# Mixture-of-experts layer in split float32: the shared down product of 30 steps, four of its five token tiles in pairs by seven block products, placed between the two routed up products

## The reference, cut to what matters

```python
x = x + gnn(layernorm(x)) + linear_attention(layernorm(x))      # 625 tokens, width 1024
xn = layernorm(x)
# 8 experts, the best 2 of each token, at most 97 tokens (CAP) each:
gate = silu(einsum('ech,ehi->eci', xg, rg)); up = einsum('ech,ehi->eci', xg, ru)   # i = 4096
eout = einsum('eci,eih->ech', gate * up, rd)
routed = zeros.at[dispatch].add(eout * w)
shared = silu(xn @ sg) * (xn @ su) @ sd                          # i = 8192, all 625 tokens
x = x + shared + routed
```

## Time and profile before

| | |
|---|---|
| median of 3 runs | 2823.61 us (2823.45 to 2825.22) |
| span of the profiled execution | 2825.1 us |
| PE busy | 2804.8 us (99% of the span), 14886 matmuls |
| DVE busy | 2233.2 us (79%) |
| ACT busy | 1489.3 us (53%) |
| DMA | 549 MB, mean 194 GB/s, 56% of the 16 engines' time |

### The profile page before, as it was taken

The page is one execution under the profiler, slowest core; times in us unless marked ns, Lnnn a source line. Parts: engine busy times, 40 slices in busy tenths (PEclk is TensorE's granted clock), DMA queues, the critical chain, the costliest instruction groups (busy, mean ns, idle before and its releaser), DMA issues.

```text
span 2825.1 us, 40627 instructions
## 1 busy us (share of the span) xinstructions
PE 2804.8 (99%) x14886; PEld 2317.9 (82%) x14886; DVE 2233.2 (79%) x2735; ACT 1489.3 (53%) x1941; POOL 55.4 (2%) x73
## 2 busy tenths in 40 slices
PE   9999999999999999999999999999999999999999
PEld 8975898788888888888888888888888888888877
DVE  8847256988888888888888888888888888888888
ACT  7722233555555555555555555555555555555563
POOL 0010000000000000000000000000000000000001
PEclk9999999999999999999999999999999999999999
DMA  4020131766666666666666666666666666666676
GB/s 114 15 83 30 60 105 45 228 217 223 223 236 223 217 212 234 222 217 214 218 214 213 215 226 211 218 216 229 219 216 216 225 219 219 224 223 217 220 263 233
DMA packets 270275, 549.06 MB, mean 194 GB/s; under 512 B 16673, under 2 KB 82465, under 8 KB 269927
## 3 DMA queue, kind: packets, MB, share of 16 engines
q1 hardware_dynamic: 265954, 532.11, 55.8%
q0 software_dynamic: 3936, 14.06, 1.6%
q10 hardware_dynamic: 162, 0.08, 0.0%
HBM read 537.49 MB, written 8.70 MB: 193 GB/s over the span
## 4 chain that ended last, share of the span: by engine, by line
PE 95%; DVE 3%; issue 0%; DMA 0%; ACT 0%; POOL 0%; POOLq 0%; DVEq 0%; SPq 0%; ACTq 0%
PE ps L1892 26%; PE ps L1896 26%; PE ps L1895 26%; PE ps L1660 3%; PE ps L1697 2%; PE ps L1699 2%; PE ps L1698 2%; PE ps L1750 2%; PE ps L1943 1%; PE ps L1784 1%; PE ps L1782 1%; PE ps L1783 1%; DVE C L990 0%; DVE c_lo L1087 0%; PE ps L1792 0%
## 5 line engine op out<-in xcount | busy, mean ns | idle before, releaser
L1439 DVE TENSOR_TENSOR c_lo<-raw,c_hi 128x1024 fp32r<-128x1024 f32 x832 | 985.1, 1219 | 99.8 <-ACT c_hi L809 99.4
L809 ACT CAST c_hi<-raw 128x1024 fp32r<-128x1024 f32 x832 | 862.9, 1050 | 157.1 <-PE ps L1896 156.7
L1892 PE MATMUL ps<-tok_hi,c_hi 128*128 128x314 f32 x1792 | 552.9, 309 | 2.8 <-DVEq L1627 1.7
L1896 PE MATMUL ps<-tok_hi,c_lo 128*128 128x314 f32 x1792 | 552.0, 308 | 0.0
L1895 PE MATMUL ps<-tok_lo,c_hi 128*128 128x314 f32 x1792 | 551.8, 308 | 0.0
L1892 PE MATMUL ps<-c_hi,xgT_hi 128*97 128x512 f32 x1024 | 404.6, 395 | 0.0
L1896 PE MATMUL ps<-c_hi,xgT_lo 128*97 128x512 f32 x1024 | 404.1, 395 | 0.0
L1895 PE MATMUL ps<-c_lo,xgT_hi 128*97 128x512 f32 x1024 | 403.3, 394 | 0.0
L1505 DVE TENSOR_TENSOR resid<-ps,resid 125x512 f32<-125x512 f32 x320 | 218.9, 686 | 178.4 <-PE ps L1896 178.2
L1892 PEld LDWEIGHTS ps<-tok_hi,c_hi 128*128 128x128 f32 x1792 | 339.4, 189 | 5.7 <-issue 1.8
L1895 PEld LDWEIGHTS ps<-tok_lo,c_hi 128*128 128x128 f32 x1792 | 339.8, 190 | 1.4
(11 more groups left out here) (251 smaller groups left out, 3526.2 us busy)
## 6 DMA issues: line engine op xcount, KB each, us to landing
raw<-in_L_ffn_rg SPq DMA_DIRECT2D x256, 512.0 KB, 4.8
raw<-in_L_ffn_ru SPq DMA_DIRECT2D x256, 512.0 KB, 4.7
raw<-in_L_ffn_rd SPq DMA_DIRECT2D x256, 512.0 KB, 6.2
raw<-in_L_ffn_sg SPq DMA_DIRECT2D x64, 512.0 KB, 5.4
raw<-in_L_ffn_su SPq DMA_DIRECT2D x64, 512.0 KB, 5.5
raw<-in_L_ffn_sd SPq DMA_DIRECT2D x64, 512.0 KB, 5.7
wl<-in_L_mix_w_qkv SPq DMA_DIRECT2D x6, 2048.0 KB, 7.9
wl<-in_L_gnn_W SPq DMA_DIRECT2D x2, 2048.0 KB, 23.1
```

The source lines that it names most:

```text
L809: nc.scalar.copy(c_hi[u % RING][:], raw_at_(q, r)[:]).then_inc(sem("hi_done"), 1 + (U - UNITS) * (u == UNITS - 1))
L1439: V.tensor_tensor(c_lo[u % RING][:], raw_at_(q, r)[:], c_hi[u % RING][:].bitcast(F32), ALU.subtract).then_inc(sem("lo_done"), 1 + (U - UNI ...
L1892: m = MM(out_, l_hi, r_hi, start=first, stop=False, skip_group_check=skip)
L1896: return MM(out_, l_lo, r_hi, start=False, stop=last, skip_group_check=skip)
```

## The change

In the 30 STEP steps:

- Token tiles 0 and 1, and 2 and 3, form two pairs. For each pair the 2 by 2 block product (two token tiles, two groups of 128 inner columns, two halves of 512 output columns) is done by seven products in place of eight. Tile 4 is done plainly, in 4 products. So there are 18 products, 54 matmuls, where there were 20 and 60.
- The factors of the scheme: DVE makes four sums of `h` (`inner_sums`, 128 by 250 each, into `hs`) and four sums of halves of the `sd` weights in the raw buffers (`down_sums`, 128 by 512 each). The shared down product has four units in place of two (15 to 18), so a step has 35. Rounding `h` goes from DVE to ACT (`inner_hi`, `inner_sums_hi`), and the subtractions are `inner_lo` and `inner_sums_lo`.
- Partial results are copied from bank to bank by ACT (`down_seed`, six of 125 by 512). One product of each pair belongs to two outputs; it is summed on its own in `p7` over all steps (`p7_add`, two of 125 by 512 a step), and the last step adds it to the odd tiles' `resid`. The ten additions to `resid` stay, as `down_add`.
- The place: the shared down product runs between `routed_up(0)` and `routed_up(1)`. `turn_inner(0)` comes between the two halves of `routed_up(1)`, then `routed_down(0, 4)`, then `turn_inner(1)`, then `routed_down(4, 8)`.
- Loads are reordered to suit; the buffers `hs`, `hs_hi`, `hs_lo` and `p7` lie where part of the descriptors' scratch area was.

Its core:

```diff
-STEP = Order(s=0, gate=(7, 15), sd=23, rd=25, a_bank=(A0, R0))
+STEP = Order(s=0, gate=(7, 19), sd=15, rd=27, a_bank=(A0, X0), sd_units=4)
@@ loads
-            blocks = {STEP: shared + inner + over + down, FIRST: shared + over + inner + down,
+            blocks = {STEP: shared + inner[0:8] + over + inner[8:16] + down, FIRST: shared + over + inner + down,
@@ ACT, hi
+                if order is STEP and u in (order.sd + 2, order.sd + 3):
+                    act.wait_ge(sem("down_sums"), count(e, q, 4, 2 * (u - order.sd - 1)))
@@ ACT, down_seed(n)
+                act.wait_ge(sem("down_ps"), count(e, q, 16, (D_P1A, D_P1B, D_P6A, D_P6B, D_P5A, D_P5B)[n]))
+                if n in (2, 3):
+                    act.wait_ge(sem("sd_added"), count(e, q, 2 * NT, (2, 1)[n - 2] + ONE))
+                if n in (4, 5):
+                    act.wait_ge(sem("p7_added"), count(e, q, 2, n - 3))
+                nc.scalar.copy(PS[to][0:TP, :], PS[DOWN_A[p]][0:TP, :]).then_inc(sem("down_seeded"), 1)
@@ ACT, step
-            for u in range(14, 21):
+            inner_hi(0)
+            inner_hi(1)
+            hi(14)
+            inner_sums_hi()
+            for u in range(15, 17):
                 hi(u)
             silu_routed(0)
-            for u in range(21, 30):
+            for u in range(17, 22):
+                hi(u)
+            down_seed(0)
+            down_seed(1)
+            hi(22)
+            for n in range(2, 6):
+                down_seed(n)
+            for u in range(23, 30):
                 hi(u)
             turned_hi(0)
             silu_routed(1)
+            for u in range(30, 32):
+                hi(u)
             turned_hi(1)
-            for u in range(30, 33):
+            for u in range(32, 35):
                 hi(u)
@@ DVE, step
-            shared_inner(1)
-            for u in range(13, 21):
+            shared_mult(1)
+            inner_sums()
+            lo(13)
+            inner_lo(0)
+            inner_lo(1)
+            lo(14)
+            inner_sums_lo()
+            for u in range(15, 17):
                 lo(u)
+            down_sums()
             routed_inner(0)
-            for u in range(21, 27):
+            for u in range(17, 20):
                 lo(u)
-            for n in range(2 * NT):
-                shared_add(n)
-                ...
+            down_add(DOWN_LAST[0], D_TA, NT - 1, 0)
+            lo(20)
+            down_add(DOWN_LAST[1], D_TB, NT - 1, 1)
+            p7_add(0)
+            p7_add(1)
+            lo(21)
+            for p in range(2):
+                down_add(DOWN_B[p], (D_P2A, D_P2B)[p], 2 * p, 0)
+            lo(22)
+            ...
+            for u in range(23, 30):
+                lo(u)
+            turned_lo(0)
+            routed_inner(1)
+            for u in range(30, 32):
+                lo(u)
             turned_lo(1)
-            for u in range(30, 33):
+            for u in range(32, 35):
                 lo(u)
@@ PE, step
             routed_up(0)
-            pe.wait_ge(sem("s_up"), count(e, q, 4, 4 + ONE))
-            routed_up(1)
+            shared_down_products()
+            pe.wait_ge(sem("sd_added"), count(e, q, 2 * NT, 5 + ONE))
+            routed_up(1, (0,))
             pe.wait_ge(sem("h_done"), count(e, q, 2, 1 + ONE))
+            pe.wait_ge(sem("sd_added"), count(e, q, 2 * NT, 2 * NT + ONE))
             turn_inner(0)
-            pe.wait_ge(sem("sh_ready"), count(e, q, 2, 2 + ONE))
-            for n in range(2 * NT):
-                shared_down(n)
+            routed_up(1, (1,))
+            routed_down(0, 4)
             pe.wait_ge(sem("h_done"), count(e, q, 2, 2 + ONE))
             turn_inner(1)
-            routed_down(0, 8)
+            routed_down(4, 8)
```

More of the change, by code:

```diff
@@ L124, in __init__ @@
         self.last_unit = [self.at(last[b - self.b0]) if self.b0 <= b < self.b0 + 4 else
-                          next(u for u in range(UNITS) if not self.shared(u) and self.block(u) == b)
+                          max(u for u in range(self.units) if not self.shared(u) and self.block(u) == b)
                           for b in range(BLK)]
@@ L143, in block @@
     def block(self, u):
[L145 removed]
+        if u <= self.s:
+            return u
+        if u < self.sd + 2 or self.sd_units == 2:
+            return u - (NPROD - 4)
+        return u - (NPROD - 4) - 2
     def raw(self, u):
@@ L482, in _, with step @@
             sp.dma_start(d, v).then_inc(sem(f"wl_in{n % 2}"), 16)
-        def step(e, q, order=STEP, part=slice(None)):
+        def step(e, q, order=STEP, part=slice(None), before=STEP):
             gate, up = sg_v[e * Q + q], su_v[e * Q + q]
@@ L509, in _ @@
         for q in range(1, Q):
-            step(0, q)
+            step(0, q, before=FIRST if q == 1 else STEP)
         with sp.Fori(1, E - 1) as e:
@@ new lines, in down_add, with p7_add @@
+            def down_add(bank, at, t, half):
+                r = resid[:, t, half * HALF:(half + 1) * HALF]
+                dve.wait_ge(sem("down_ps"), count(e, q, 16, at))
+                V.tensor_tensor(r, PS[bank][0:TP, :], r, ALU.add).then_inc(sem("sd_added"), 1)
+            def p7_add(p):
+                dve.wait_ge(sem("down_ps"), count(e, q, 16, (D_P7A, D_P7B)[p]))
+                V.tensor_tensor(p7[:, p, :], PS[DOWN_D[p]][0:TP, :], p7[:, p, :], ALU.add).then_inc(sem("p7_added"), 1)
@@ L1514, in step @@
                     lo(u)
+                for p in range(2):
+                    for half in range(2):
+                        r = resid[:, 2 * p + 1, half * HALF:(half + 1) * HALF]
+                        link(V.tensor_tensor(r, p7[:, p, :], r, ALU.add))
                 routed_inner(0)
@@ L1908, in routed_up @@
                                   c_hi[u % RING][:, c], c_lo[u % RING][:, c], k == 0, k == KT - 1,
-                                  used=(order is FIRST and b == 0 and i == 0 and k == 0))
+                                  used=(order.after_down if b == order.down_before and i == 0 and k == 0 else 0))
                         if k % 2:
@@ L1944, in turn_inner @@
                            ident[0:CAP, 0:CAP])
-                    if b == 1 and k == 0 and order is STEP:
-                        m.then_inc(sem("unit_used"), 1)
                 m.then_inc(sem("t_done"), 1)
@@ L1986, in routed_down, with down_product @@
                                   c_hi[u % RING][:, c], c_lo[u % RING][:, c], k == 0, k == 7)
-                    m.then_inc(sem("unit_used"), 1 + (U - UNITS) * (u == UNITS - 1))
+                    m.then_inc(sem("unit_used"), 1 + (U - order.units) * (u == order.units - 1))
+            def down_product(bank, l_hi, l_lo, u, half, first, last=True, added=None):
+                c = slice(half * HALF, (half + 1) * HALF)
+                return three(PS[bank][0:TP, :], l_hi, l_lo, c_hi[u % RING][:, c], c_lo[u % RING][:, c], first, last,
+                             skip=not first if added is None else added)
```

159 lines of the change are left out of this document (136 added, 23 removed).

## The result

The changed kernel takes 2949.2 us (2947.98 to 2950.54), the kernel before 2823.6 beside it: a ratio of 1.044, 95% interval 1.0428 to 1.0458, so 4.4% slower. The forecast was 2940 us in a range of 2850 to 3000. The profiled execution has a span of 2946.2 us, 121.1 more than before: 4.04 us for each of the 30 steps.

What follows compares the result with a forecast made beforehand. The prediction took PE, busy without a gap at 72.3 us a step, as the bound. Saving and costs, -41.7 + 57 + 41.1 + 58, gave +114 to +116 us on 2823.6: 2940 us, range 2850 to 3000.

Steps and rivals of the forecast that it cites:

- cost 1: End of products(1) to routed_down: DVE's queue takes 37.0 us against PE's 35.1, so PE waits 1.9 us a step.
- cost 2: Behind the transposes of turn_inner(1): product k = 4 waits for turned_lo(1), 1.37 us a step.
- cost 3: Next step's first units come late: PE waits 0.6 us at unit 0, 1.4 at unit 2, at 29 boundaries.
- The saving: Six matmuls of 512 columns fewer on PE in each of 30 steps: 1.39 us a step, 41.7 in all.
- (a): Rival: DVE's new work is absorbed and only the transposes cost; 2823 us, or 2819; chance 0.12 including a middle.
- (b): Rival: PE's clock falls in the steps' new gaps, costing 1 to 3 us a step; some 3000 us; chance 0.15.
- (c): Rival: ACT stands waiting at seeds, hi(17), hi(18); waits add up, 3 to 4 us more a step; 3040 us; chance 0.08.

Runs made afterwards that it cites:

- b_54: The kernel before with six matmuls a step left out (tile 4 lacks its second inner group), nothing else of the change; 2782.4 us, ratio 0.9853.
- a_tuned3_60: a_tuned3 with the six saved matmuls put back in each of the 30 steps; 2855.7 us, ratio 1.0110.
- a_60: The changed kernel with six matmuls a step put back (tile 4's first product done twice); 2947.4 us, ratio 1.0438.
- b_turn_late: The kernel before with only turn_inner(1) moved between k = 3 and k = 4 of routed_down; 2934.9 us, ratio 1.0389.
- a_tuned3: a_tuned2 with one unit of the routed down product moved ahead of the second turned piece on ACT and DVE; 2816.1 us, ratio 0.9970.
- a_seeds_early: The changed kernel with ACT making the first two seeds behind hi(18) instead of hi(21); 2959.6 us, ratio 1.0476.
- a_tuned: The changed kernel with turn_inner(1) behind k = 1, seeds spread on ACT, and DVE's queue reordered, some work behind routed_inner(1); 2847.2 us, ratio 1.0083.
- a_tuned2: a_tuned with DVE's two late additions moved ahead of routed_inner(1); 2850.4 us, ratio 1.0091.
- a_tuned_no_p7: a_tuned with the two p7_add of each step left out (output lacks one product of each pair); 2847.8 us, ratio 1.0085.

## Why the prediction was right

Times a step, the wait forecast beside the wait measured:

| | forecast | measured |
|---|---|---|
| six matmuls less | -1.39 | -1.39 |
| cost 1, the stretch up to routed_down | 1.9 | 1.32, all at P6 |
| cost 2, behind turn_inner(1) | 1.37 | 1.38 |
| cost 3, unit 0 and unit 2 of the next step | 0.6 + 1.4 | 0.40 + 1.46 |
| not in the sum: slower restarts | | 0.71 |
| at five changes of expert inside the steps | 0 | 1.1 more each |
| LAST, once | 0 | 4 |

30 x (-1.39 + 1.32 + 1.38 + 0.71) + 29 x 1.86 + 5 x 1.1 + 4 = 124 us, and the two spans differ by 121.1. Of the 3 us between them 1.7 are time that the kernel before loses at three changes of expert, and 1.2 the first STEP, which comes sooner (see the clock below).

The mechanism and two of three costs were as forecast. That the number fits to 9 us is in part luck: cost 1 was put 17 us too high, and some 31 us of restarts, changes of expert and LAST were not in the sum at all. (The chance of about 0.8 for the range was put too high as well: the parts named there add up to some 0.74.)

- **The saving** is the term of the sum: b_54 gave -41, a_tuned3_60 39.5. That it bought nothing in the changed kernel (a_60) is no contradiction, because in the forecast too cost 1 was PE's stretch against DVE's: what PE saves there, it waits.
- **Cost 2** was read off the timeline of before link by link and came out to 0.01 us. b_turn_late shows it, and cost 3, on a kernel without the rest of the change.
- **Cost 3** was worked out from the distances of the earlier trace rows and is right in both waits of an ordinary step. What I missed is a loop turn. SP and ACT go around their loops over the experts at five of the steps. There ACT rounds unit 0 late, and unit 0 of the step that follows waits 1.5 to 1.9 us in place of 0.40, while unit 2 waits a little less, 1.31. ACT before an ordinary step and before such a one, with the issue of the load of unit 0's block, and ACT's instructions of the loop itself (line 1018):

```profile
1631.04 2.94 ACT L839 CAST c_hi<-raw 128x1024 fp32r<-128x1024 f32 x3
1633.89 1.05 ACT L719 CAST c_hi<-raw 128x1024 fp32r<-128x1024 f32 x1
...
1703.51 0.39 SPq L526 DMA_DIRECT2D raw<-in_L_ffn_sg  x1
1707.23 2.94 ACT L839 CAST c_hi<-raw 128x1024 fp32r<-128x1024 f32 x3
1712.88 1.99 ACT L719 CAST c_hi<-raw 128x1024 fp32r<-128x1024 f32 x2 [2.71 <-PE ps L2046]
...
L1018 ACTq COMPARE_BRANCH  x1: 45/45/45, 1707.2 to 1707.2; - x1
L1018 ACTq FUSED_REGOPS  x1: 50/50/50, 1712.7 to 1712.7; - x1
```

  Between ACT's branch and the first instruction behind it lie 5.5 us, and unit 0 is rounded 0.17 us later, after 2.71 us of idle time. The releaser that the row names is not what ACT waited for: in the ordinary step the same rounding starts 2.1 us behind the first matmul of k = 4, and here 4.9 us behind it, with PE that much further on. Nor is it the load: that is issued late too, 6.7 us behind the last rd load where it otherwise follows after 1.15, but it lands after 3.8 us, at 1707.3. The kernel before has the same turn (2.4 to 2.7 us) and the same late issue (6.6 to 7.0 us) at the same five places, but there ACT has 2.2 us to spare before unit 0 in every step, and the load comes some 23 us ahead of its step in place of 11 to 12. Why the turn takes longer in the changed kernel was not tried. In a_tuned3 the waits at unit 2 behind these turns are 0.7 to 1.3 us by the trace's records, among others of 0.6, and at one of them (1643.67) ACT does wait for this load.
- **LAST.** The prediction took p7's four additions in the last step as 0, with 0 to 2 us possible. In the changed kernel PE waits 2.94 us there for routed_inner(0), which stands behind them on DVE, and later 1.24; in b_turn_late, which has no p7, the same two waits are 0.27 and 1.44. So the additions cost some 2.7 us.
- **Cost 1** is the term of the sum that was mis-sized: 1.9 us forecast, 1.32 measured, 17 us over the 30 steps. DVE's stretch was 36.3 us for 36.9, the durations being those estimated (0.41 to 0.42 us for 250 columns, 0.69 for 512), and the wait came at P6 alone, none at routed_down. (DVE's busy time rose by 6.5 us a step, where 8.0 was forecast.) That the wait is of one queue is supported by a_seeds_early (it moved to P5, and grew) and by a_60 (it went when PE had as much to do). No run takes work away from DVE in this stretch with the rest of the changed kernel as it is.
- **The 0.71 us outside the sum**: about 0.3 is the first matmul behind each of the four waits, whose distance to the next is 0.31 us and not 0.232 (1682.11 to 1682.41, above), or 0.22 and not 0.145 for 314 columns. The rest lies in distances that are longer by 0.05 to 0.14 us, which I did not trace to a cause.
- **The rivals.** (a), DVE's work is absorbed: it fell as a forecast, since PE waited at P6 and at both units. But what spoke for it, that DVE's time of a step is not used up, held: a_tuned3 does the same work in 133 us less, and two p7_add a step less changed neither a_tuned nor a_tuned2. It was the order that kept DVE's free time from being used. (b), the clock: the window above shows 1.00, that is 2.4 GHz, with three waits of 1.1 to 1.3 us by the records in a step and one of 0.24, or 1.3 to 1.7 at the five loop turns, and from 485 us on the clock of the changed kernel does not fall before its last microsecond. The premise was weaker than it looked, though. The very wait of 2.93 us in FIRST after which the clock of the kernel before fell to 0.50 is in the changed kernel too, and there it stayed at 1.00; so it did behind the wait of 2.94 us in LAST. In a_seeds_early, on the other hand, it fell in a STEP, behind a wait of 1.80 us:

```profile
548.00:550.00 2.00, 0.00 (x0) 0.00 (x0) 1.76 (x9) 0.00 (x0) 0.00 (x0) 1.00 0.92 322
550.00:552.00 2.00, 1.59 (x10) 1.24 (x11) 2.00 (x3) 1.00 (x2) 0.80 (x1) 1.00 0.62 229
...
2028.00:2030.00 2.00, 1.57 (x7) 1.60 (x8) 1.90 (x3) 0.00 (x0) 0.00 (x0) 0.72 1.04 377
2030.00:2032.00 2.00, 2.00 (x9) 2.00 (x9) 1.90 (x3) 1.14 (x2) 0.00 (x0) 0.50 0.59 211
```

  (The first two rows are of the changed kernel, the others of a_seeds_early.) Of the 14 profiled executions 8 show the fall behind FIRST's wait and 6 don't, with the same length of wait. So the length of one wait does not decide it in this case, and the prediction's argument that no wait would be as long was not enough against this rival, although it did not come true. The fall of 6.8 us in the kernel before cost it 1.15 us: its first STEP begins that much later. The section on HAM oscillation that the prediction names from the Trainium skill (TensorE: Matmul & The Clock Gate) works its rule out on waits of some 3 to 5 us between bursts; the waits of the steps here are shorter and do not test it, and the falls behind 1.80 and 2.93 us came after shorter waits than those. (c), waits that add up: none did in the changed kernel.

Where the prediction's reasoning was thin is the word "fits". It said that 67 us of DVE fit beside 71 of PE only if DVE hardly ever waits, and left it there. The runs show that 66 us of DVE fit into a step of 71.8 us, if no instruction stands at the head of its queue waiting for PE while others behind it are ready.

## What to carry to other kernels

Before an operation is moved, list what stood between it and its consumer: four transposes moved behind four more units of matmuls cost 110 us, more than twice what the whole scheme saves. When an in-order engine is both the bound and idle in the same step, look for the instruction at the head of its queue that is pinned to another engine, and put ready work in front of it, as far back as its own consumer allows; work ahead of such an instruction may cost nothing at all (a_tuned_no_p7), while one unit a step moved from behind it to ahead of it was worth 34 us (a_tuned3). And a saving on an engine that has begun to wait is worth nothing until the waits are gone: the same six matmuls were worth 41, 0 and 39.5 us in three kernels with the same reference.

## What the runs showed of the hardware

- TensorE's granted clock stayed at 1.00 through four waits of 0.4 to 1.5 us in every ordinary step of 76 us. Behind one wait of 2.93 us, the same in all kernels, it fell to 0.50 in 8 profiled executions and stayed at 1.00 in 6.
- A turn of ACT's loop took 2.4 to 2.7 us from the branch to the next instruction in the kernel before, and 5.5 to 5.9 us in the changed one. The engine works off meanwhile what it had been given, 2.94 us of copies above, and then stands idle.
- The first matmul of 512 columns behind a wait is followed by the next after 0.30 to 0.34 us, where 0.232 is the distance in a dense row: each wait costs some 0.07 us more than its own length.
- A copy of 125 by 512 from bank to bank on ACT takes 0.57 us (forecast 0.58): two took 1.06 us together.

```profile
1677.59 3.89 ACT L839 CAST c_hi<-raw 128x1024 fp32r<-128x1024 f32 x4 [0.45 <-DVE raw L1599]
1681.39 1.06 ACT L907 COPY ps<-ps 125x512 f32<-125x512 f32 x2
```

  These two rows, of the changed kernel, are also P6's wait as ACT has it: hi(18) to hi(21), then the two seeds, and P6 starts at 1682.11.
